# Expert routing moved earlier beside a shared expert, with one multiply moved from VectorE to ScalarE

## The chip, the cores and the metric

One NeuronCore of a Trainium2 chip runs the whole program. The metric is the time of one execution on the device, in microseconds (us); lower is better. A run is the median of several executions.

## What is computed

64 samples of 64 rows and 512 columns (4096 rows, here called tokens, of width 512). First each sample is multiplied by one of 8 matrices and gets a bias; then comes a mixture of experts with a shared expert, and the input is added:

```
h = einsum('bct,bcd->bdt', x, cond_weights[itok]) + fside[itok][:, :, None]   # 64x64 matrices
scores = sigmoid(h @ gate_weight.T)                    # 16 experts
biased = scores + expert_bias
# of 4 groups of 4 experts the 2 with the largest sum of their top two; of those the top 4 experts
w = 2.5 * scores[top4] / sum(scores[top4])
out = x + sum_e w_e * (silu(h @ g_e.T) * (h @ u_e.T)) @ d_e.T     # 4 of 16 experts per token
        + (silu(h @ sg.T) * (h @ su.T)) @ sd.T                    # shared expert, every token
```

The hidden width of each expert is 256. All is float32; a product of the experts is made as three passes over high and low parts.

## The kernel before, in words

A tile is 128 tokens. The program has three stages, and all five engines run written-out instruction lists that meet at semaphores.

**Conditioning stage (some 80 us), loop `for n in range(NT + 2)`, 32 tiles.** GpSimd (POOL) reads two entries of `itok_row` per tile and copies the two 64x64 matrices out of `cond_sb` into `cw_ring` (L526, L534); after tile 4 it makes constants with `late_consts` (L490 and on), among them `token_q`, `lane_q` and `tile_q`. TensorE (PE) multiplies (L755), ScalarE (ACT) adds the bias (L622), SyncE (SP) stores the rows in `h_rows` (L394), PE transposes them (L730), ACT copies the result (L626), PE makes the router's logits (L772). Ahead of it PE runs `WARM_UP` = 8 matmuls on ones (L716). SP issues the first loads in the order `cond_sb`, `itok_row`, others (L375 to L380).

**Shared expert (some 80 to 233 us), steps n = 0 to 31, one tile each.** In step n PE runs `gate_up(n)` (12 matmuls into `psGU`), transposes `hid` of tile n-1 (L730), then whatever the tables of numbers put in this step, then `down(n-2)` (6 matmuls into `psY`). ACT runs `copy_y(n-3)` (L653), `copy_xT(n+1)` (L613), SiLU (L691), `copy_hidT(n-1)` (L644) and, in the steps of `HIGHS`, a high part of a piece of weights (L603). VectorE (DVE) runs `split_x(n+1)` (L1257), then `route_part(n)`, then `mix(n)` (L1280), then `split_hid(n-1)` (L1270).

`route_part` is the routing in 15 numbered parts, one per step, then the reading of two word tables, and then 16 groups of "entries". Each group covers two columns of tokens and takes three VectorE operations on float16: a one-hot of the tile number (`entry`, L1232 by way of L907), a one-hot of the lane (`lane1h`, which lies in `x_ring`, by way of L907), and `entry` times the token number `token_q` (L1235). PE then multiplies `lane1h` by `entry` into the bank `psM` (`fill_slots`, L850), 8 matmuls a group; the sum over all groups is the table of token numbers for each place of each expert tile. `ENTRY_STEPS` says in which step each group is made, 14 to 24, and PE fills it one step later. `fill_idx` (step 25, L1245 and on) turns the table into row indices, `idx_all`. After that POOL gathers rows for the first 14 expert tiles (`gather`, L545), in places that `FIRST_GATHER` = 23 and `GATHERS` set: behind the accumulation of shared tile 23's result into `out` (L558), and so on. Before a gather of tiles 8 and up POOL waits until the shuffle of the tile that used its buffer has landed.

SP has one queue. In it stand the loads of the experts' weights, 1.5 MB each (`load_raw`, L399), whose places `RAW_LOADS` sets and which wait for the low parts (`LOWS`, VectorE, L1240) of the weights that they overwrite; and the shuffles (L415 and L418), which bring gathered rows, two tiles at a time, into the layout that VectorE's transposition `turn_x` (L1264) reads. ACT's queue has the copies of x into `out` (`copy_x`, L597), 1 MB each.

**Routed experts (some 233 to 858 us).** 143 tiles in a loop with the same step, weights of 16 experts one after another; results are scattered with addition (L550).

The word tables (which weights each engine prepares when) are made by PE as sums into `psM` (L784, L801, L802) and read by VectorE (L1176, L1177, L1181). Since they use the bank of the fill, the first fill has to wait until they are read.

## Time and profile before

| what | us |
|---|---|
| median of 3 runs | 878.07 (875.76 to 878.13) |
| the profiled execution's own time | 876.7 |
| its span | 875.0 |
| TensorE busy in the span | 854.5 |
| VectorE, ScalarE, GpSimd busy | 497.5, 401.8, 439.8 |

The profile is of one execution. The span runs from its first to its last instruction; the 1.7 us around it are launch and end. In rows of the page and of the trace "busy" is time inside instructions, overlapping ones counted once; what stands behind an arrow in brackets released the engine after it had been idle. PE's matmuls are pipelined, so that its rows overlap.

### The profile page before, as it was taken

To read this page: it belongs to the slowest core of one execution; us is meant where nothing else is said; L and a number is where in the kernel's file an instruction comes from. 1 tells how busy PE (TensorE), PEld (TensorE's weight loads), DVE (VectorE), ACT (ScalarE), POOL (GpSimd) and SP (SyncE) were. 2 spreads that over 40 slices of the span, in tenths; PEclk is the share of its full clock that TensorE was granted. 3 is DMA by queue.
4 is the path that set the end of the run, shared out by engine and by line. 5 is a ranking of instruction groups with operands and counts; after the bars stand their busy time and mean duration, and the time that the engine had idled before them with its cause. 6 is when DMAs were issued, how large, how long until landed. Compare 5 with 4: busy or idle time off the path is not lost.

```text
span 875.0 us, 19555 instructions
## 1 busy us (share of the span) xinstructions
PE 854.5 (98%) x4136; PEld 693.9 (79%) x4137; DVE 497.5 (57%) x1071; ACT 401.8 (46%) x852; POOL 439.8 (50%) x402
## 2 busy tenths in 40 slices
PE   8999999999899999999999999999999999999994
PEld 6778887888788888888888888888878878887883
DVE  1457677886464454564446644756647456464540
ACT  4675443534443333553445534645545355453331
POOL 4430211115446656656656647656656575765333
PEclk8999999999999999999999999999999999999998
DMA  7983576758999999989999999999898999999644
GB/s 235 345 291 133 134 126 170 173 98 207 262 241 263 218 180 197 183 200 285 226 187 173 204 268 214 184 298 232 197 275 174 280 241 235 240 183 193 119 61 62
DMA packets 147092, 179.06 MB, mean 205 GB/s; under 512 B 30986, under 2 KB 104210, under 8 KB 144658
## 3 DMA queue, kind: packets, MB, share of 16 engines
q0 software_dynamic: 37296, 86.95, 50.3%
q1 hardware_dynamic: 108258, 80.41, 35.7%
q10 hardware_dynamic: 1408, 10.49, 3.5%
q14 instruction: 112, 0.92, 0.4%
q8 instruction: 18, 0.29, 0.1%
HBM read 82.48 MB, written 65.04 MB: 169 GB/s over the span
## 4 chain that ended last, share of the span: by engine, by line
PE 79%; DMA 7%; issue 5%; SPq 3%; POOL 2%; DVE 0%; ACT 0%; POOLq 0%; DVEq 0%; ACTq 0%
PE psGU L824 44%; PE psY L824 22%; PE psY L755 4%; PE psH L730 4%; PE psGU L772 3%; DMA out<-y_ring,idx_all 3%; DMA tok_ring<-h_rows,idx_all 2%; SPq L415 2%; PE psT L730 2%; DMA w_ring<-tok_ring 2%; POOL out L550 1%; POOL out L558 1%; SPq L418 0%; PE psM L850 0%; SPq L436 0%
## 5 line engine op out<-in xcount | busy, mean ns | idle before, releaser
L824 PE MATMUL psGU<-split_w,xT_hi 128*128 (+1 forms) x1400 | 433.2, 391 | 3.3 <-DVE xT_lo L1257 3.3
L550 POOL DMA_INDIRECT out<-y_ring,idx_all x143 | 234.8, 1642 | 207.4 <-SPq L454 190.1
L824 PEld LDWEIGHTS psGU<-split_w,xT_hi 128*128 128x128 f32 x1400 | 263.0, 188 | 61.1 <-issue 5.3
L824 PE MATMUL psGU<-split_w,xT_lo 128*128 (+1 forms) x700 | 274.1, 392 | 0.0
L824 PE MATMUL psY<-split_w,hidT_hi 128*128 (+1 forms) x700 | 233.0, 414 | 0.2 <-issue 0.2
L691 ACT ACTIVATE aT<-psGU 128x256 f32<-128x256 f32 x175 | 67.3, 385 | 264.0 <-PE psGU L824 262.4
L1257 DVE TENSOR_TENSOR xT_lo<-psT,xT_hi 128x512 fp32r<-128x512 f32 x143 | 98.8, 691 | 148.0 <-ACT xT_hi L613 133.7
L545 POOL DMA_INDIRECT tok_ring<-h_rows,idx_all x143 | 147.7, 1033 | 52.9 <-issue 43.2
L653 ACT ACTIVATE y_ring<-psY 128x512 f32<-128x512 f32 x175 | 104.0, 594 | 143.9 <-PE psY L824 127.3
L824 PEld LDWEIGHTS psGU<-split_w,xT_lo 128*128 128x128 f32 x700 | 131.7, 188 | 28.0
L824 PE MATMUL psY<-split_w,hidT_lo 128*128 (+1 forms) x350 | 138.2, 395 | 0.0
L824 PEld LDWEIGHTS psY<-split_w,hidT_hi 128*128 128x128 f32 x700 | 118.5, 189 | 16.2 <-issue 0.7
L1282 DVE SCALAR_TENSOR_TENSOR aT<-aT,w_ring,psGU 128x256 f32<-128x256 f32 x143 | 66.9, 468 | 86.7 <-ACT aT L691 86.7
L1264 DVE STREAM_TRANSPOSE psT<-x_ring 128x512 f32<-128x512 f32 x143 | 102.5, 717 | 6.1 <-DMA w_ring<-tok_ring 6.1
L558 POOL DMA_DIRECT2D out<-y_ring x32 | 28.2, 882 | 131.8 <-ACT y_ring L653 131.7
L613 ACT ACTIVATE xT_hi<-psT 128x512 fp32r<-128x512 f32 x143 | 84.7, 592 | 5.2 <-DVE psT L1264 5.2
L824 PEld LDWEIGHTS psY<-split_w,hidT_lo 128*128 128x128 f32 x350 | 65.8, 188 | 15.0
L1297 DVE TENSOR_TENSOR split_w<-raw_w,split_w x42 | 51.5, 1227 | 41.1 <-ACT split_w L663 38.2
L1270 DVE TENSOR_TENSOR hidT_lo<-psH,hidT_hi 128x256 fp32r<-128x256 f32 x175 | 73.1, 417 | 1.0 <-ACT hidT_hi L644 1.0
L730 PEld LDWEIGHTS psH<-ident,aT 128*128 128x128 f32 x350 | 48.9, 140 | 26.0 <-DVE aT L1280 2.8
L730 PE MATMUL psH<-ident,aT 128*128 128x128 f32 x350 | 66.9, 272 | 2.4 <-DVE hidT_lo L1270 2.4
L644 ACT ACTIVATE hidT_hi<-psH 128x256 fp32r<-128x256 f32 x175 | 66.4, 379 | 1.7 <-PE psH L730 1.7
(177 smaller groups left out, 488.9 us busy)
## 6 DMA issues: line engine op xcount, KB each, us to landing
x_ring<-tok_ring SPq DMA_DIRECT2D x284, 128.0 KB
raw_w<-ffn_w SPq DMA_DIRECT2D x17, 1536.0 KB, 11.7
h_rows<-tok_ring SPq DMA_DIRECT2D x32, 256.0 KB, 3.6
out<-y_ring POOLq DMA_DIRECT2D x32, 256.0 KB
x_ring<-x SPq DMA_DIRECT2D x24, 256.0 KB, 4.6
tok_ring<-h_rows,idx_all POOLq DMA_INDIRECT x143
out<-y_ring,idx_all POOLq DMA_INDIRECT x143
x_ring<-x ACTq DMA_DIRECT2D x8, 256.0 KB, 3.7
```

Source lines behind the costliest of these rows:

```text
L545: pool.indirect_dma_start(tok_ring[:, r % RING, :], None, h_rows[:, :], bass.IndirectOffsetOnAxis(idx_all[:, r:r + 1], 0)).then_inc(gather ...
L550: pool.indirect_dma_start(out[:, :], bass.IndirectOffsetOnAxis(idx_all[:, r:r + 1], 0), y_ring[:, r % YRING, :], None, compute_op=ALU.add) ...
L613: act.activation(xT_hi[:, t.slot % 2, :], xT, ACT.Copy).then_inc(xhi_ready, 1)
L644: act.activation(hidT_hi[:, t.slot % 2, :], psH[:, 0:I], ACT.Copy).then_inc(hidhi_ready, 1)
L653: act.activation(y_ring[:, s, :], psY[t.slot % 2][:], ACT.Copy).then_inc(y_ready, 1)
L691: act.activation(silu[:, t.slot % 2, :], psGU[t.slot % 2][:, 0:I], ACT.Silu).then_inc(silu_ready, 1)
L730: mm = pe.transpose(dst[:, k * P:(k + 1) * P], src[:, k * P:(k + 1) * P], ident[:])
L824: mm = pe.matmul(dst, a[:, slot, c], w(at + col + k * H), start=(k == 0 and a is high and at == 0), stop=(k == parts - 1 and a is low))
L1257: v.tensor_tensor(xT_lo[:, t.slot % 2, :], xT, xT_hi[:, t.slot % 2, :].bitcast(F32), ALU.subtract).then_inc(xT_ready, 1)
L1264: v.transpose(psT[t.slot % 2][:].rearrange("p (k b j) -> p k j b", k=HK, j=QUADS), x_duo[:, t.slot // DUO_TILES, :, t.slot % DUO_TILES, :] ...
L1270: v.tensor_tensor(hidT_lo[:, t.slot % 2, :], psH[:, 0:I], hidT_hi[:, t.slot % 2, :].bitcast(F32), ALU.subtract).then_inc(hidT_ready, 1)
L1282: ins = v.scalar_tensor_tensor(out=hid[:, half, :], in0=gate, scalar=w_ring[:, w_slot, bass.ds(expert, 1)], in1=up, op0=ALU.mult, op1=ALU. ...
```

## The change

`route_part` now takes its work from `ROUTE_STEPS`, by name: the same parts in fewer steps, and the parts that lead to the tokens' places (`slots`, `top_slots`, `places`) come ahead of those that lead to the words. The 16 groups of entries are made in steps 9 to 20. The multiplication by token numbers leaves VectorE: ScalarE scales the lane one-hots, two activations a group (`scale_lanes`), with a column of `token_no` as scale. The word tables use the banks `psT[0]` and `psT[1]`. `fill_idx` is in step 22, the gathers begin behind shared tile 20, low parts and weight loads have other steps, `WARM_UP` is 12, and SP loads `itok_row` ahead of `cond_sb`.

```diff
+ROUTE_STEPS = {0: ("groups",), 1: ("top_experts",), 2: ("ties", "counts"), 3: ("weights",), 4: ("ranks",),
+               5: ("take_turns",), 6: ("starts",), 7: ("slots", "keys"), 8: ("top_slots",), 9: ("places",),
+               10: ("words",), 11: ("columns",), 12: ("tables",), 14: ("read_words",), 15: ("read_sp_words",),
+               22: ("fill_idx",)}
-ENTRY_STEPS = {14: (0,), 15: (1, 2), 16: (3,), 17: (4, 5), 18: (6,), 19: (7, 8), 20: (9,), 21: (10, 11),
-               22: (12,), 23: (13, 14), 24: (15,)}
-FILL_IDX = 25
+ENTRY_STEPS = {9: (0,), 11: (1,), 13: (2, 3), 14: (4,), 15: (5,), 16: (6, 7), 17: (8, 9), 18: (10, 11), 19: (12, 13),
+               20: (14, 15)}
-PE_POS_FFN = {1: 2, 4: 3}
-PE_WORDS, READ_WORDS = 12, 13
-PE_SP_WORDS, READ_SP_WORDS = 13, 14
+PE_POS_FFN = {1: 2, 3: 3}
+PE_WORDS = 13
+PE_SP_WORDS = 14
-LOWS = {25: ((1, 0),), 26: ((1, 1), (1, 2)), 27: ((2, 0),), 29: ((2, 1),), 31: ((2, 2),)}
-RAW_LOADS = {14: 1, 15: 2, 23: 3, 28: 4}
-WARM_UP = 8
+LOWS = {21: ((1, 0),), 23: ((1, 1),), 24: ((1, 2),), 26: ((2, 0),), 29: ((2, 1),), 31: ((2, 2),)}
+RAW_LOADS = {14: 1, 15: 2, 23: 3, 31: 4}
+WARM_UP = 12
-FIRST_GATHER = 23
-GATHERS = {23: (0, 1), 24: (2, 3), 25: (4, 5), 26: (6, 7), 28: (8, 9), 29: (10, 11), 30: (12, 13)}
+FIRST_GATHER = 20
+GATHERS = {20: (0, 1), 21: (2, 3), 22: (4, 5), 23: (6, 7), 25: (8, 9), 26: (10, 11), 27: (12, 13)}
...
-            sp.dma_start(cond_sb[:], cond_w).then_inc(cond_loaded, 16)
             sp.dma_start(itok_row[:], itok.unsqueeze(0)).then_inc(itok_loaded, 16)
+            sp.dma_start(cond_sb[:], cond_w).then_inc(cond_loaded, 16)
...
-                iota(token_q[:, 0:half, :], [[P, half], [0, TOPK]], -N // 2, 1)
-                iota(token_q[:, half:NT, :], [[P, half], [0, TOPK]], 1, 1)
+                iota(token_no[:, 0:half], [[P, half]], -N // 2, 1)
+                iota(token_no[:, half:NT], [[P, half]], 1, 1)
...
-                elif n in (NT - 1, NT):
-                    copy_xT(tile_at(n - (NT - 1)), n - (NT - 1))
+                if n in (NT - 2, NT - 1):
+                    copy_xT(tile_at(n - (NT - 2)), n - (NT - 2))
...
+            def scale_lanes(g):
+
+                act.wait_ge(places_ready, 2 * (g + 1))
+                s = g % ENTRY_RING
+                half = PAIRS // DUO // ENTRIES
+                for k in range(ENTRIES):
+                    lanes = lane1h[:, s, k * half:(k + 1) * half, :, :].rearrange("p d l q -> p (d l q)")
+                    act.activation(lanes, lanes, ACT.Copy, scale=token_no[:, g * ENTRIES + k:g * ENTRIES + k + 1]
+                                   ).then_inc(entry_ready, 1)
...
                     copy_hidT(t + -1, None if n is None else n - 1)
+                for g in ENTRY_STEPS.get(n, ()):
+                    scale_lanes(g)
...
-                pe.wait_ge(words_ready, 1)
-                pe.wait_ge(order_ready, 1)
-                pe.matmul(psM[0:1, 0:NRP], e_cols[:, USED:USED + 1], first[:], start=True, stop=False)
+                pe.matmul(psT[1][0:1, 0:NRP], e_cols[:, USED:USED + 1], first[:], start=True, stop=False)
...
-                pe.wait_ge(entry_ready, g + 1)
+                pe.wait_ge(entry_ready, ENTRIES * (g + 1))
                 if g == 0:
-                    pe.wait_ge(sp_words_ready, 1)
+                    pe.wait_ge(pos_read, NB)
...
-                tokens = token_q[:].rearrange("p c k -> p (c k)")[:, pairs]
-                tt(entry[:, s], every(tile_q[:]), duos(slot_tile[:, pairs], NRP), ALU.is_equal)
-                tt(lane1h[:, s], every(lane_q[:]), duos(slot_lane[:, pairs], P), ALU.is_equal)
-                settle()
-                v.tensor_tensor(entry[:, s], entry[:, s], duos(tokens, NRP), ALU.mult).then_inc(entry_ready, 1)
+                v.tensor_tensor(entry[:, s], every(tile_q[:]), duos(slot_tile[:, pairs], NRP), ALU.is_equal
+                                ).then_inc(places_ready, 1)
+                v.tensor_tensor(lane1h[:, s], every(lane_q[:]), duos(slot_lane[:, pairs], P), ALU.is_equal
+                                ).then_inc(places_ready, 1)
```

On ScalarE, step 17 of the shared expert before (the first row is `copy_y`, `xT_hi` is `copy_xT`, the row with `aT` is SiLU, `split_w` a high part):

```order
L653 ACTIVATE y_ring<-psY 128x512 [waits scattered2,down_done]
L613 ACTIVATE xT_hi<-kept_w 128x512 [waits gu_done]
L691 ACTIVATE aT<-psGU 128x256 [waits hid_ready,gu_done]
L644 ACTIVATE hidT_hi<-psH 128x256 [waits down_done,hid_xposed]
L603 ACTIVATE split_w<-raw_w 128x1024 [waits xT_ready,raw_loaded]
L597 DMA out<-x 16x16384
```

The same step now, number 17, with two groups to scale:

```order
L656 ACTIVATE y_ring<-psY 128x512 [waits scattered2,down_done]
L616 ACTIVATE xT_hi<-kept_w 128x512 [waits gu_done]
L704 ACTIVATE aT<-psGU 128x256 [waits hid_ready,gu_done]
L647 ACTIVATE hidT_hi<-psH 128x256 [waits down_done,hid_xposed]
L689 ACTIVATE x_ring<-x_ring,token_no 128x512 [waits places_ready]
L689 ACTIVATE x_ring<-x_ring,token_no 128x512
L689 ACTIVATE x_ring<-x_ring,token_no 128x512 [waits places_ready]
L689 ACTIVATE x_ring<-x_ring,token_no 128x512
L606 ACTIVATE split_w<-raw_w 128x1024 [waits xT_ready,raw_loaded]
L600 DMA out<-x 16x16384
```

Four activations, the first of each pair behind a wait for VectorE (`places_ready`), now stand between `copy_hidT` and the high part, and so ahead of the next step's `copy_y` and `copy_xT`.

On VectorE, a step with two groups before (`xT_lo` is `split_x`, the row with `aT` is `mix`):

```order
L1257 TENSOR_TENSOR xT_lo<-kept_w,xT_hi 128x512 [waits xhi_ready]
L907 TENSOR_TENSOR entry<-tile_q,slot_tile 128x1152 [waits table_done]
L907 TENSOR_TENSOR x_ring<-lane_q,slot_lane 128x1024
L1235 TENSOR_TENSOR entry<-entry,token_q 128x1152 [waits dve]
L907 TENSOR_TENSOR entry<-tile_q,slot_tile 128x1152 [waits table_done]
L907 TENSOR_TENSOR x_ring<-lane_q,slot_lane 128x1024
L1235 TENSOR_TENSOR entry<-entry,token_q 128x1152 [waits dve]
L1280 TENSOR_TENSOR aT<-aT,psGU 128x256 [waits hid_xposed,silu_ready]
```

And now:

```order
L1269 TENSOR_TENSOR xT_lo<-kept_w,xT_hi 128x512 [waits xhi_ready]
L1244 TENSOR_TENSOR entry<-tile_q,slot_tile 128x1152 [waits table_done]
L1246 TENSOR_TENSOR x_ring<-lane_q,slot_lane 128x1024
L1244 TENSOR_TENSOR entry<-tile_q,slot_tile 128x1152 [waits table_done]
L1246 TENSOR_TENSOR x_ring<-lane_q,slot_lane 128x1024
L1292 TENSOR_TENSOR aT<-aT,psGU 128x256 [waits hid_xposed,silu_ready]
```

The multiplication is gone, and with it the wait for the operation before it. There are six steps of this kind in a table that had five, and five of them, 16 to 20, follow on one another.

## Rows read from the trace of the kernel before

**Rows 1.** Waits, whole span: who waited for whom, total us, times, longest

```profile
DVE psT L1264 <- DMA w_ring<-tok_ring: 6.1, 1, 6.1
```

**Rows 2.** Chain that ended last, 205 to 245 us: start, us, what

```profile
216.35 13.74 DMA w_ring<-tok_ring
...
231.70 0.41 PE psH L730 x2
...
233.97 3.86 PE psGU L824 x12
```

**Rows 3.** Stretches: PE busy (instructions), granted clock, DMA share, GB/s

```profile
222.00:229.00 7.00, 7.00 (x33) 1.00 1.10 256
229.00:232.00 3.00, 0.59 (x5) 1.00 1.23 201
...
233.00:236.00 3.00, 3.00 (x9) 0.50 1.24 222
```

**Rows 4.** Timelines of POOL and SP around the gathers, and issues to landing

```profile
207.19 1.11 POOL L545 DMA_INDIRECT tok_ring<-h_rows,idx_all  x1 [0.54 <-issue]
...
210.37 0.34 SPq L399 DMA_DIRECT2D raw_w<-ffn_w  x1
...
out<-x ACTq DMA_DIRECT2D x1, 5.6
```

**Rows 5.** Groups of ScalarE and VectorE, shared expert: busy, mean ns

```profile
L653 ACT ACTIVATE y_ring<-psY 128x512 f32<-128x512 f32 x28 | 16.8, 600 | 34.5 <-PE psY L824 34.5
L613 ACT ACTIVATE xT_hi<-kept_w 128x512 fp32r<-128x512 f32 x24 | 15.0, 623 | 0.0
...
L603 ACT ACTIVATE split_w<-raw_w 128x1024 fp32r<-128x1024 f32 x5 | 5.3, 1061 | 0.0
...
L1235 DVE TENSOR_TENSOR entry<-entry,token_q 128x1152 f16<-128x1152 f16 x16 | 12.1, 758 | 0.6
```

**Rows 6.** ScalarE's bias activation, whole span: min/median/max ns

```profile
L622 ACT ACTIVATE tok_ring<-psY,bias_tok x32: 678/687/691, 8.7 to 78.1; 128x512 f32<-128x512 f32 x32
```

**Rows 7.** VectorE's timeline in one step with two groups

```profile
159.68 0.69 DVE L1257 TENSOR_TENSOR xT_lo<-kept_w,xT_hi 128x512 fp32r<-128x512 f32 x1 [0.90 <-ACT xT_hi L613]
160.29 0.75 DVE L907 TENSOR_TENSOR entry<-tile_q,slot_tile 128x1152 f16<-128x1152 f16 x1
...
162.36 0.75 DVE L907 TENSOR_TENSOR entry<-tile_q,slot_tile 128x1152 f16<-128x1152 f16 x1
```

**Rows 8.** Tile 17's split on VectorE and its products in the chain; SiLU of tiles 16, 17

```profile
155.37 0.68 DVE L1257 TENSOR_TENSOR xT_lo<-kept_w,xT_hi 128x512 fp32r<-128x512 f32 x1
...
158.50 2.72 PE psGU L824 x12
...
155.73 0.38 ACT L691 ACTIVATE aT<-psGU 128x256 f32<-128x256 f32 x1 [1.61 <-PE psGU L824]
...
161.26 0.39 ACT L691 ACTIVATE aT<-psGU 128x256 f32<-128x256 f32 x1 [1.61 <-PE psGU L824]
```

**Rows 9.** Chain at the start: start, us, what

```profile
1.28 3.13 DMA itok_row<-itok
...
6.29 1.10 PE psY L755 x2
...
10.21 0.85 PE psT L730 x4
...
19.21 0.95 PE psY L755 x2
```

**Rows 10.** Timelines at the start: PE's warm-up, ScalarE, POOL

```profile
1.26 3.40 PE L716 MATMUL psM<-ones 128*128 128x128 f32 x16 [1.26 <-DVE ones L928]
...
8.69 0.69 ACT L622 ACTIVATE tok_ring<-psY,bias_tok 128x512 f32<-128x512 f32 x1
...
17.36 0.52 POOL L534 COPY cw_ring<-cond_sb 64x64 f32 x2 [1.36 <-issue]
```

**Rows 11.** Stretches at the start: PE busy, clock, DMA share, GB/s

```profile
8.00:9.00 1.00, 1.00 (x2) 0.50 0.69 264
```

More of the change, by code:

```diff
@@ L311, in build @@
         sp_words_ready = sem("sp_words_ready")
+        places_ready = sem("places_ready")
         entry_ready = sem("entry_ready")
@@ L373, in _ @@
         def _(sp):
+            sp.dma_start(itok_row[:], itok.unsqueeze(0)).then_inc(itok_loaded, 16)
             sp.dma_start(cond_sb[:], cond_w).then_inc(cond_loaded, 16)
-            sp.dma_start(itok_row[:], itok.unsqueeze(0)).then_inc(itok_loaded, 16)
             sp.dma_start(itok8[:], itok.partition_broadcast(NS)).then_inc(fside_loaded, 16)
@@ L783, in sums @@
                     for k, (column, rows_e) in enumerate(terms):
-                        mm = pe.matmul(psM[0:1, at:at + rows_e.shape[1]], column, rows_e[:, :],
+                        mm = pe.matmul(psT[0][0:1, at:at + rows_e.shape[1]], column, rows_e[:, :],
                                        start=(k == 0), stop=(k == len(terms) - 1))
@@ L1175, in read_words @@
                 v.wait_ge(words_summed, 1)
-                v.tensor_copy(order[:], psM[0:1, 3 * NR:3 * NR + E + SPLITS + 2]).then_inc(order_ready, 1)
-                v.tensor_copy(words[:], psM[0:1, 0:3 * NR]).then_inc(words_ready, 1)
+                v.tensor_copy(order[:], psT[0][0:1, 3 * NR:3 * NR + E + SPLITS + 2]).then_inc(order_ready, 1)
+                v.tensor_copy(words[:], psT[0][0:1, 0:3 * NR]).then_inc(words_ready, 1)
             def read_sp_words():
                 v.wait_ge(sp_words_summed, 1)
-                put(v.tensor_copy(sp_rows[:], psM[0:1, 0:NRP]))
+                put(v.tensor_copy(sp_rows[:], psT[1][0:1, 0:NRP]))
                 settle()
@@ L1193, in token_slots @@
                 in_batches = slot_e[:].rearrange("p (b c e) -> p b c e", c=BC, e=E)
-                ts(start, start, float(P), 1.0, ALU.mult, ALU.add)
+                ts(first_slot[:], start, float(P), 1.0, ALU.mult, ALU.add)
                 settle()
-                tt(per_chunk(slot_e[:], E), per_chunk(pos[:], E), over_chunks(start, NT), ALU.add)
+                tt(per_chunk(slot_e[:], E), per_chunk(pos[:], E), over_chunks(first_slot[:], NT), ALU.add)
                 settle()
@@ new lines, in route_part @@
+                for part in ROUTE_STEPS.get(n, ()):
+                    if part == "groups":
+                        route_groups(NB - 1)
+                    elif part == "top_experts":
+                        top_experts(NB - 1)
+                    elif part == "ties":
+                        chosen_experts(NB - 1)
+                    elif part == "counts":
+                        read_positions(NB - 2)
+                        count_slots(NB - 1)
+                    elif part == "weights":
+                        route_weights(NB - 1)
+                    elif part == "ranks":
+                        expert_ranks()
+                    elif part == "take_turns":
+                        expert_turns()
+                    elif part == "starts":
+                        expert_starts()
+                    elif part == "slots":
+                        token_slots()
+                    elif part == "keys":
+                        expert_keys()
+                    elif part == "top_slots":
+                        top_slots()
+                    elif part == "places":
+                        slot_places()
+                    elif part == "words":
+                        expert_words()
+                    elif part == "columns":
+                        expert_columns()
+                    elif part == "tables":
+                        tile_tables()
+                    elif part == "read_words":
+                        read_words()
+                    elif part == "read_sp_words":
+                        read_sp_words()
+                    elif part == "fill_idx":
+                        fill_idx()
```

44 lines of the change are left out of this document (3 added, 41 removed).

## The prediction

> **What bounds the kernel now.** I read in the order: busy shares, waits, the chain of waits, then timelines of the places that the chain names. TensorE is busy 854.5 of 875.0 us, so only what TensorE itself does, its half-speed time, and the few places where it stands still can change the time. Two of these lie where the change works.
>
> The first is the passage from the shared expert to the routed ones. VectorE waits 6.1 us, once, for the shuffle of the first gathered pair [rows 1]; in the chain that shuffle (its last DMA, `w_ring<-tok_ring`) takes 13.74 us from issue at 216.35 to landing at 230.1, and TensorE starts again at 231.70 [rows 2]. In the stretch 229 to 232 TensorE is busy 0.59 of 3.00 us: it stands 2.4 us. Behind that the granted clock is 0.50 (1.2 GHz) in 233 to 236, and full before [rows 3]; the 12 products at 233.97 take 3.86 us where 2.73 is usual [rows 2]. Against an even step of 4.34 us the SiLUs of tiles 31 and 32 come 2.1 us late each, **4.2 us** in all, of which half is the wait and half the clock.
>
> Why does the shuffle land so late? SP issued a 1.5 MB load of weights at 210.37 [rows 4], and the shuffle stands behind it in SP's queue. From that issue to the landing it is 19.7 us. The first gather was issued at 207.19 [rows 4].
>
> The second place is the start. TensorE's warm-up ends at 4.66 [rows 10], the first product starts at 6.29 [rows 9], and the clock, full until then, is 0.50 in 8 to 9 [rows 11]. Four transposes take 0.85 there [rows 9]; at full clock they take 0.44. The gap of 1.6 us before the first product is what went ahead of the fall.
>
> **The change, part by part.**
>
> *Earlier gathers, loads and shuffles.* The places are ready in `fill_idx` of step 22 instead of 25, and the first gather stands behind shared tile 20 instead of 23: three steps of 4.34 us or a little over, so the gather goes at about 194 to 195. The weight load that goes ahead of the shuffle waits for the last low part of turn 1, now in step 24 instead of 26: some 10 us earlier, near 200. With the same 19.7 us the shuffle lands near 220. It meets more traffic now: the last 1 MB copy of x, which took 5.6 us [rows 4] and was over before the load, now runs beside it. So 220 to 226. VectorE could use it late by 2.4 us less than it did before without TensorE stopping, that is until 227.7, and until 228.8 with the delay found below. The wait goes, and the half clock with it: **-4.2 us**; bounds 0 (lands as late as before) and -4.2. The next thing that could be late is the following pair, needed two steps (8.7 us) later, which lands some 2 us behind the first.
>
> *Multiply from VectorE to ScalarE.* VectorE is spared 16 x 758 ns [rows 5], but it was not the bound: in a two-group step it was about as long as TensorE. ScalarE gets 32 activations of 128x512. Their price is not in the trace. From below: a plain copy from the same memory, 623 ns. From above: an activation that also reads a column of numbers per partition, 687 ns [rows 6], taken without any overlap. Consecutive ones overlap by 0.1 us, so I take 0.59 us each (687 less 0.1), since this one reads such a column too; ends 0.52 and 0.69. The Trainium skill ("ScalarE: Activation LUTs", What ACT_TABLE_LOAD costs) gives 186 ns plus 0.833 ns an element and 93 ns more for each column operand, and an overlap of 93 ns back to back. By that, as an estimate, one would take 0.61 us and the sum would be 0.2 us higher; the plain copy's 623 ns agrees with it (613).
>
> What counts is not the sum but a ring of waits, new in this kernel: `split_x` on VectorE, then the two groups, then ScalarE's scaling of the second group, its high part, `copy_y`, `copy_xT`, and `split_x` again. The split is 0.61 us; a group of three operations took 2.07 [rows 7], without the multiply 1.35, so two are 2.70; two scalings 1.18; the high part 0.95 (1061 ns less the overlap); `copy_y` 0.49 and `copy_xT` 0.53 [rows 5]; semaphores 0.2. That is **6.66 us** with a high part (steps 17, 18, 19) and 5.7 without (steps 16 and 20). TensorE's step with two fills takes 5.5 us (SiLU 155.73 to 161.26 [rows 8]). The ring falls behind by 3 x 1.2 + 2 x 0.2 = 3.9 us. The cover is what a split is ahead of its product: tile 17's ended at 156.0 and its product began at 158.50 [rows 8], 2.5 us, up to 2.8 after steps with fewer groups. So TensorE waits about 1.2 us near step 20: **+1.2 us**. With 0.52 the lag is about 2.6 and nothing is left; with 0.69 it is near 5.8 and 3.4 us are left. These waits are shorter each than the one that went ahead of a fall of the clock.
>
> *Steps merged, tables in other banks.* VectorE's heaviest early steps (`ties` with `counts`, 3.4 us of work; `slots` with `keys`, 2.8) stay inside 4.34 us with the 1.3 us of split, mix and split. TensorE does the same 128 fill matmuls and the same sums; I cost this at nothing. What hides it is VectorE's lead; without that an overlong step would cost its excess, at most 0.4 us. The order of experts is read one step later, so the first weight load is too, some 5 us; it landed 7 us before ScalarE's first use, and 2 to 3 us are left.
>
> *Accumulations behind gathers.* POOL's gathers of tiles 8 to 13 wait for shuffles, and now stand ahead of the accumulations of shared tiles 26, 27 and 28 instead of 29 to 31. Normal if the shuffles land by about 226; costed at nothing (rival D).
>
> *Start.* The DMA of `itok_row` took 3.13 us for 0.2 KB [rows 9]; it stood behind 256 KB in the same queue. First in it, it lands perhaps 0.9 us earlier, and POOL's copies with it. Four more warm-up matmuls take 0.4 us at half clock, 0.2 at full: TensorE is busy until 5.3 to 6.4, about where the first product starts, so the gap that went ahead of the fall closes. If the clock then stays up, the first transposes start not at 10.21 but when ScalarE's first tile is done, at 9.4 (8.69 + 0.69 [rows 10]), and tile 5 could start at 16.4 instead of 19.21 [rows 9]: 2.8 us. But POOL made tile 5's matrices only from 17.36 to 17.88 [rows 10], behind its constants; with 0.9 us from the load and 0.3 from shorter constants that is 16.7, so 2.4 us at most. A new gap opens (TensorE waits for ScalarE's first tile from 8.0 to 9.4), so the clock may fall anyway, later. I take **-1.9 us**, between 0 and -2.8.
>
> Sum: -4.2 + 1.2 - 1.9 = -4.9 us, from 876.7 of the profiled execution to 871.8. That execution is below the median of the runs (878.07); the mean of the four times is 877.2. I move the result by half a microsecond and more to that: **872.4 us**. All cases below are moved by the same 0.6. About 0.3% (2.6 us) is what a measurement of this kernel can tell from no change.
>
> **Rivals.**
>
> A. *The start gives nothing*: the clock falls all the same, or POOL's constants hold tile 5. For it: the new gap before the first transposes. Against: TensorE's clock was full through the warm-up. 876.7 - 4.2 + 1.2 + 0.6 = 874.3. Chance 0.15.
>
> B. *The ring of waits costs its upper end*, 3.4 us: 876.7 - 4.2 + 3.4 - 1.9 + 0.6 = 874.6. The Trainium skill's table (same page, Rules for kernel authors) says to multiply on VectorE and not on ScalarE; the trace has the price of the exchange, one operation of 758 ns for two of some 690. Chance 0.12.
>
> C. *The shuffle is still late*, at 230, because copy, gathers and load share the DMA engines (share already 1.10 in 222 to 229 [rows 3]). One microsecond of wait and the half clock stay, 3.1 of 4.2: 875.5. Chance 0.08.
>
> D. *Slower: POOL's accumulations are held up.* If the shuffle lands at 232 or later, gather 8 holds the accumulation of tile 26; issued 3 us and landed 9 us after the shuffle, at 241, it is late for `copy_y` of tile 30, which needs its buffer near 236.5, and TensorE stands twice, each time with a half clock after it: 3.2 + 2.1, then 2.3 + 2.1, in all 9.7 in place of 4.2. 876.7 + 5.5 + 1.2 - 1.9 + 0.6 = 882.1. It decides from a landing at 232. For it: 8 MB in 30 us. Against: the load starts 10 us earlier. Chance 0.04.
>
> E. *Both small terms at their good ends* (ring 0, start -2.8): 870.3. Chance 0.11.
>
> **How the numbers follow.** The forecast (871 to 874) has 0.5. The range 869.0 to 876.5 takes in A, B, C and E with a microsecond for how runs differ, and leaves out D and a part of the tails. Faster by over 0.3% (under 875.4): all but D, half of C and parts of A and B, 0.84. Within 0.3%: 0.12. Slower: 0.04.
>
> **What would show it.** After the change VectorE's transposition no longer waits for `w_ring<-tok_ring` near 225, and the clock is full from 20 to the last tiles. TensorE stands about 1 us around step 20 (180 to 186), released by VectorE, with `split_x` waiting for ScalarE's `copy_xT`. The first gather is near 193, the shuffle lands before 227. The fifth tile of conditioning starts near 17. Wrong would be: a wait at the passage that stays, waits of ScalarE's `copy_y` for `out` near 236, or TensorE waits in steps 13 to 20 of more than 3 us.

## The result and the profile after

The change made the kernel faster: median **872.52 us** (869.14 to 877.28, 17 runs) against 878.07 us (873.78 to 884.29, 17 runs). The ratio is 0.9939, with a 95% interval of 0.9914 to 0.9963. The profiled execution has an own time of 872.52 us and a span of 870.8 us, 4.2 us below that of before in both.

The head of the page after:

```profile
span 870.8 us, 19587 instructions
...
PE 851.7 (98%) x4144; PEld 691.9 (79%) x4145; DVE 484.6 (56%) x1055; ACT 421.2 (48%) x884; POOL 440.2 (51%) x402
```

TensorE is still the bound. It is busy 2.8 us less than before for nearly the same instructions, so part of the gain is time at the full clock. The rest is time in which it no longer stands.

Stretches of the kernel after (columns: stretch, PE busy, PEld, DVE, ACT, POOL, granted clock, DMA share, GB/s):

```profile
8.00:11.00 3.00, 2.83 (x13) 1.48 (x13) 2.30 (x12) 2.54 (x6) 1.97 (x9) 1.00 1.01 363
...
180.00:190.00 10.00, 9.32 (x54) 7.30 (x53) 8.13 (x17) 6.09 (x13) 2.31 (x3) 1.00 0.62 142
...
229.00:232.00 3.00, 3.00 (x15) 2.47 (x14) 1.60 (x3) 2.45 (x5) 2.40 (x3) 1.00 1.10 294
...
233.00:236.00 3.00, 3.00 (x16) 2.50 (x15) 1.70 (x5) 2.63 (x5) 1.56 (x3) 1.00 1.03 310
```

Against [rows 3]: in 229 to 232 TensorE is now busy all 3.00 us, and the clock is full in 233 to 236. Against [rows 11]: the clock stays full behind 8, though TensorE is idle for 0.2 us of 8 to 11. In 180 to 190 it is idle for 0.7 us, which is the ring of waits, below.

The passage after: VectorE's timeline, then POOL's and SP's.

```profile
222.85 0.69 DVE L1269 TENSOR_TENSOR xT_lo<-kept_w,xT_hi 128x512 fp32r<-128x512 f32 x1 [1.57 <-issue]
223.46 0.72 DVE L1276 STREAM_TRANSPOSE psT<-x_ring 128x512 f32<-128x512 f32 x1
```

```profile
193.61 1.65 POOL L548 DMA_INDIRECT tok_ring<-h_rows,idx_all  x1 [0.53 <-DMA out<-y_ring]
...
221.84 1.06 POOL L548 DMA_INDIRECT tok_ring<-h_rows,idx_all  x1 [7.00 <-DMA w_ring<-tok_ring]
...
224.43 1.01 POOL L561 DMA_DIRECT2D out<-y_ring  x1
```

```profile
199.99 0.35 SPq L402 DMA_DIRECT2D raw_w<-ffn_w  x1
200.55 3.08 SPq L418 DMA_DIRECT2D x_ring<-tok_ring  x4
203.68 3.77 SPq L421 DMA_DIRECT2D w_ring<-tok_ring  x1
```

The 6.1 us of [rows 1] are gone: the transposition follows the split without a wait. The first gather is issued at 193.61, the weight load at 199.99, and gather 8, which waits for the shuffle, goes at 221.84. So the shuffle landed near 221.8, which is 21.8 us after the load's issue (before: 19.7).

The start after, in the chain:

```profile
1.26 5.37 PE psM L731 x24
6.64 0.86 PE psY L770 x2
...
9.28 0.66 PE psT L745 x4
...
16.41 0.72 issue
17.13 1.10 PE psY L770 x2
```

The warm-up ends where the first product starts, and the first transposes start at 9.28 instead of 10.21. Tile 5 starts at 17.13 instead of 19.21 [rows 9], after a stop of 0.7 us.

The ring of waits, first on VectorE, then on ScalarE, then TensorE's waits in 85 to 240 us:

```profile
173.45 0.69 DVE L1269 TENSOR_TENSOR xT_lo<-kept_w,xT_hi 128x512 fp32r<-128x512 f32 x1 [2.69 <-ACT xT_hi L616]
...
180.03 0.69 DVE L1269 TENSOR_TENSOR xT_lo<-kept_w,xT_hi 128x512 fp32r<-128x512 f32 x1 [2.68 <-ACT xT_hi L616]
```

```profile
175.45 2.60 ACT L689 ACTIVATE x_ring<-x_ring,token_no 128x512 f16<-128x512 f16 x4 [1.49 <-DVE x_ring L1246]
177.96 1.04 ACT L606 ACTIVATE split_w<-raw_w 128x1024 fp32r<-128x1024 f32 x1
...
179.38 0.62 ACT L616 ACTIVATE xT_hi<-kept_w 128x512 fp32r<-128x512 f32 x1
```

```profile
PE psH L745 <- DVE hidT_lo L1282: 0.5, 2, 0.3
PE psGU L837 <- DVE xT_lo L1269: 0.4, 1, 0.4
```

From split to split 6.58 us pass in a step with two groups and a high part, each split waiting 2.7 us for `copy_xT` behind ScalarE's scalings. TensorE waits for VectorE three times, at 177.5, 180.8 and 184.1 in steps 20 and 21, 0.9 us in all.

**One ruler for all kernels.** TensorE paces the SiLUs of `gate_up`, so the starts of three of them part the first quarter of the program. The SiLU of shared tile 0 shows the start, that of tile 29 the steps with fills, that of the first routed tile the passage. These are the three rows of the kernel after (ScalarE's timeline):

```profile
82.62 0.38 ACT L704 ACTIVATE aT<-psGU 128x256 f32<-128x256 f32 x1 [1.14 <-PE psGU L837]
...
220.11 0.38 ACT L704 ACTIVATE aT<-psGU 128x256 f32<-128x256 f32 x1 [1.61 <-PE psGU L837]
...
233.08 0.39 ACT L704 ACTIVATE aT<-psGU 128x256 f32<-128x256 f32 x1 [1.64 <-PE psGU L837]
```

The same rows of every profiled execution, in us; the last column is the time from the third row to the end of the span:

| Kernel | SiLU of tile 0 | from there to tile 29 | from there to routed tile 0 | from there to the end |
|---|---|---|---|---|
| before | 84.5 | 136.1 | 17.2 | 637.1 |
| before again (e12) | 88.8 | 136.1 | 15.2 | 639.0 |
| after | 82.6 | 137.5 | 13.0 | 637.7 |
| e1, warm-up 8 | 82.9 | 137.6 | 13.1 | 639.0 |
| e2, matrices loaded first | 83.3 | 137.3 | 13.0 | 636.8 |
| e3, multiply on VectorE | 82.8 | 135.6 | 13.0 | 634.3 |
| e4, high parts moved | 82.9 | 135.8 | 13.0 | 636.5 |
| e5, gathers late | 82.4 | 137.3 | 13.0 | 635.4 |
| e6, before, load later | 88.5 | 136.1 | 13.0 | 642.7 |
| e7, constants later | 81.8 | 137.2 | 13.0 | 635.8 |
| e8 = e4 and e7 | 81.9 | 135.6 | 13.0 | 636.5 |
| e9, before, warm-up 12 | 83.2 | 136.0 | 15.5 | 635.5 |
| e10 = e1 and e2 | 86.0 | 137.3 | 13.0 | 635.8 |
| e11 = e3 and e7 | 81.8 | 135.6 | 13.0 | 638.0 |

Each column moves only with the part of the program that it spans. Between before and after it is -1.9, +1.4 and -4.2 us, together -4.8 at the first routed tile; the routed stage gave back 0.6. That last column varies by up to 4.7 us between kernels whose routed stage is the same, so no part of a result is read from it.

**The clock of the runs.** Each timed run has a span and a mean granted clock too, and (1 - clock) x span is the clock time that it was not granted. Not all of that is a loss. In every profile the clock also falls once TensorE has made its last product (in after the products end at 859.6 and the half clock begins at 863.1), and this end alone is 3.8 us of the figure in after, which is all that its profile has, and 3.2 to 4.9 us in the others. So only differences between kernels say something, and they do not say where in the program the clock fell.

| Kernel | runs | mean clock (lowest to highest) | not granted |
|---|---|---|---|
| before, beside e1 to e11 | 73 | 0.9920 (0.986 to 0.994) | 7.0 us |
| after | 17 | 0.9946 (0.992 to 0.996) | 4.7 us |
| e1 to e5, e7, e8, e11 together | 68 | 0.9946 (0.991 to 0.997) | 4.7 us |
| e6 | 10 | 0.9921 (0.988 to 0.994) | 6.9 us |
| e10 | 12 | 0.9929 (0.992 to 0.994) | 6.2 us |
| e9 | 10 | 0.9900 (0.985 to 0.996) | 8.8 us |

Two more runs of before, over 1.5% above its fastest, are left out. The means of the times differ by 4.3 us (877.0 for the 73 of before, 872.8 for the 17 of after, not all on one chip); 2.4 us of that is clock. Of the 73 runs of before 23 have a clock of 0.991 or less and average 880.4 us, the other 50 average 875.5; none of the 17 runs of after is that low.

### The profile page after: what moved, and what is told of

Same layout as the page of the kernel before. It is cut to its first block, busy times and chain, and to the rows that moved or that the text cites. A ratio compares the mean times of both kernels' runs of the same rounds, so it can differ in the third digit from the quotient of the medians.

```text
span 870.8 us, 19587 instructions
## 1 busy us (share of the span) xinstructions
PE 851.7 (98%) x4144; PEld 691.9 (79%) x4145; DVE 484.6 (56%) x1055; ACT 421.2 (48%) x884; POOL 440.2 (51%) x402
## 4 chain that ended last, share of the span: by engine, by line
PE 85%; issue 4%; DVE 2%; ACT 2%; DMA 2%; SPq 1%; POOL 1%; DVEq 1%; ACTq 0%
PE psGU L837 48%; PE psY L837 24%; PE psH L745 4%; PE psY L770 3%; PE psGU L787 3%; DMA out<-y_ring,idx_all 2%; PE psT L745 2%; POOL out L553 1%; SPq L418 1%; ACT x_ring L689 1%; DVE entry L1244 1%; PE psM L731 1%; DVE x_ring L1246 1%; ACT y_ring L656 0%; ACT xT_hi L616 0%
## 5 line engine op out<-in xcount | busy, mean ns | idle before, releaser
L548 POOL DMA_INDIRECT tok_ring<-h_rows,idx_all x143 | 150.2, 1051 | 57.6 <-issue 42.6
L837 PE MATMUL psY<-split_w,hidT_lo 128*128 (+1 forms) x350 | 137.6, 393 | 0.0
```

Source lines behind the costliest of these rows:

```text
L548: pool.indirect_dma_start(tok_ring[:, r % RING, :], None, h_rows[:, :], bass.IndirectOffsetOnAxis(idx_all[:, r:r + 1], 0)).then_inc(gather ...
L837: mm = pe.matmul(dst, a[:, slot, c], w(at + col + k * H), start=(k == 0 and a is high and at == 0), stop=(k == parts - 1 and a is low))
```

## The experiments

### The start: warm-up and the order of two loads

One reading has to be put right first. The clock's column shows 1.00 from the start of the span, but the trace's first record of the clock comes only at 4.1 us in before, 6.4 in after and 12.8 in e10; what the column shows ahead of it was not measured. Durations were: the warm-up's matmuls in before and in e10 (lowest, median and highest ns):

```profile
L716 PE MATMUL psM<-ones x16: 274/421/579, 1.3 to 4.4; 128*128 128x128 f32 x16
```

```profile
L731 PE MATMUL psM<-ones x16: 421/421/582, 1.3 to 4.6; 128*128 128x128 f32 x16
```

One takes 274 ns at full clock; the median of the warm-up is 421 in every profile. So all these kernels begin at half clock, and it comes up within the first microseconds, in e10 only at 12.8. In before it is up at 4.1 and falls at 7.5, behind the stop of 1.6 us.

The change makes two edits at the start. The first two runs undo one each, in the changed kernel.

```diff
-WARM_UP = 12
+WARM_UP = 8
```

> The changed kernel with 8 warm-up matmuls instead of 12. Theory (the four more matmuls close the gap ahead of the first product, and that keeps the clock up): TensorE idles some 0.5 to 1 us after the warm-up, which is less than before the change (1.6), because itok_row now comes first; if that is still too much, the clock falls to 0.5 within the first 15 us and tile 5 of conditioning starts near 19 instead of 17.1, +1.5 to +2 us on the span's passage to the shared expert. Rival (the earlier matrices did it, not the warm-up): the clock stays full and tile 5 starts at 17.1 as in the changed kernel, no difference.

Measured: 872.01 us (868.89 to 875.62), ratio to before 0.9941 (0.9908 to 0.9974). TensorE's timeline of e1:

```profile
5.38 1.41 PE L770 MATMUL psY<-x_ring,cw_ring 128*128 128x512 f32 x2 [0.34 <-POOL cw_ring L537]
```

The matrices are there at 5.4, so that even the short warm-up leaves a gap of only 0.3 us, and the clock is full from 6.0 us on. Tile 0's SiLU comes 0.2 us later than in the kernel after.

```diff
-sp.dma_start(itok_row[:], itok.unsqueeze(0)).then_inc(itok_loaded, 16)
 sp.dma_start(cond_sb[:], cond_w).then_inc(cond_loaded, 16)
+sp.dma_start(itok_row[:], itok.unsqueeze(0)).then_inc(itok_loaded, 16)
```

> The changed kernel with the load of cond_sb ahead of itok_row again, 12 warm-up matmuls kept. Theory (the warm-up holds the first product back anyway, but POOL's copies set when tile 5 can start): POOL's first copy goes back from 4.45 to 5.6 us, its copy for tile 5 from 16.5 to some 17.2 to 17.6, and tile 5's product from 17.1 to about 18; the clock stays full. +0.7 to +1.1 us. Rival (constants are behind a wait that the swap does not move, or the longer stop at tile 5 lets the clock fall): 0, or +2.5 or more.

Measured: 871.71 us (868.64 to 875.08), ratio 0.9936 (0.9904 to 0.9968). POOL's first copy goes at 5.55 instead of 4.45 and tile 5's matrices come later too: TensorE stops 1.3 us before tile 5 and does it at 17.84. The 12 warm-up matmuls run until the first product starts, and the clock is full from 6.1 us on. Tile 0's SiLU is 0.7 us later.

In these two profiles either edit alone was enough for a full clock. The changed kernel without both is e10:

```diff
-WARM_UP = 12
+WARM_UP = 8
-sp.dma_start(itok_row[:], itok.unsqueeze(0)).then_inc(itok_loaded, 16)
 sp.dma_start(cond_sb[:], cond_w).then_inc(cond_loaded, 16)
+sp.dma_start(itok_row[:], itok.unsqueeze(0)).then_inc(itok_loaded, 16)
```

> The changed kernel with both edits of the start undone: 8 warm-up matmuls and cond_sb loaded first. Theory (either edit alone keeps TensorE's gap ahead of the first product short; with neither the gap of 1.6 us is back): the clock falls to 0.5 somewhere in the first 25 us and the first SiLU of the shared expert comes at 84.5 or later instead of 82.6; passage and ring of waits as in the changed kernel. Median 1.5 to 3 us above the changed kernel. Rival (the fall is chance and has nothing to do with the gap): clock full, first SiLU at 83.3 or less, same time as the changed kernel.

Measured: 875.02 us (871.68 to 877.93), ratio 0.9947 (0.9922 to 0.9973). The chain at its start:

```profile
6.24 2.04 PE psY L770 x2
...
11.28 0.85 PE psT L745 x4
```

After a wait of 1.2 us two products take 2.0 us where 0.95 is usual, and four transposes 0.85 where 0.44 is: half clock until 12.8 us. Against the expectation it did not fall: no warm-up matmul is faster than 421 ns, so it had not come up yet. By the chains this costs 1.7 us up to tile 6 (its products start at 21.20 instead of 19.46). Tile 0's SiLU comes 3.3 us later than in the kernel after, and the other 1.6 us are a second stretch at half clock, from 81.1 to 84.5, with no stop of TensorE ahead of it (stretch, PE busy, granted clock, DMA share, GB/s):

```profile
78.00:81.00 3.00, 2.99 (x29) 1.00 1.11 350
81.00:84.00 3.00, 3.00 (x11) 0.51 0.30 87
```

What brought that one on is open. Without it the SiLU would have come near 84.4, just under the 84.5 that was expected. The 12 timed runs have clocks of 0.992 to 0.994, on average 1.5 us more not granted than the runs of after. They do not show where: in the profiled one the mean clock holds the stretch at 81 and not the start, which lies ahead of the first record. The two ratios, 0.9947 and 0.9939, are too close to be told apart by themselves.

The mirror image is the kernel before with the long warm-up:

```diff
-WARM_UP = 8
+WARM_UP = 12
```

> The kernel before with 12 warm-up matmuls instead of 8, nothing else. Theory (the gap of 1.6 us between warm-up and first product went ahead of the fall of the clock; filling it is enough): the clock stays full in the first 20 us, tile 5 of conditioning starts near 18 (held by POOL) instead of 19.2, -1.2 us. Rival (it took the earlier itok_row): the clock falls as before and tile 5 starts at 19.2 or later.

Measured: 879.05 us (871.81 to 884.63), ratio 1.0027 (0.9992 to 1.0062). In the profile it did what was expected: tile 0's SiLU at 83.2, full clock at the start. But that execution (871.81 us, clock 0.996) was the fastest of ten, and the other nine have clocks of 0.985 to 0.993. The expectation holds for the start of one execution and fails for the time. No run shows where the nine lost theirs.

The kernel before, unchanged, was looked at once more:

> The kernel before, unchanged, for a second profile of its start and of its passage. Theory: the clock falls to 0.5 somewhere in the first 25 us, first SiLU at 84 to 89; VectorE waits 4 us or more for the first shuffle, which lands near 230 behind a weight load of 210, and TensorE stands 2 us or more. Rival (the first profile was a chance): clock full and first SiLU at 83.3 or less; or no stop at the passage.

Measured: 880.85 us. Stretches and chain of e12 at the start:

```profile
14.00:18.00 4.00, 2.46 (x17) 1.83 (x16) 0.00 (x0) 1.78 (x5) 2.31 (x3) 1.00 0.87 267
18.00:20.00 2.00, 1.62 (x6) 1.12 (x7) 0.00 (x0) 0.44 (x1) 0.91 (x4) 0.82 0.22 80
20.00:24.00 4.00, 4.00 (x14) 2.86 (x13) 0.00 (x0) 1.20 (x4) 1.76 (x9) 0.50 0.37 131
...
28.00:32.00 4.00, 4.00 (x27) 3.48 (x25) 0.00 (x0) 2.41 (x5) 0.93 (x4) 0.81 1.01 347
```

```profile
16.45 1.92 issue
```

Here the clock did not fall at the front. It fell after the stop of 1.9 us at tile 5, where POOL's matrices come late, and stayed down until 29.5 (0.81 in 28 to 32). So before has two places at its start at which the clock can go, and in this execution the second cost more (SiLU at 88.8) than the first did in the other (84.5). e6, another kernel with before's start, shows the same fall after 2.0 us. At the front the clock stayed full in both, behind stops of 1.4 us (e12) and 0.8 us (e6), though the program up to there is before's. So the same start goes differently from one execution to the next, and one profile each of e1, e2, e9 and e10 fits the account of the gap but does not prove it.

### POOL's constants

If the stop at tile 5 is POOL's constants, starting them three tiles later must close it.

```diff
-PAIR_TABLES = 4
+PAIR_TABLES = 7
```

> The changed kernel with POOL's constants made after tile 7's matrices instead of after tile 4's. Theory (POOL's 7 us of constants hold tile 5 by 0.7 us): POOL has tiles 5 to 7 ready by 12.5, tile 5 starts at 16.4 instead of 17.1, tile 8 waits only for its buffer, and the first SiLU of the shared expert comes 0.7 us earlier. Rival (tile 8 is now held by the same 7 us): TensorE waits at tile 8, and nothing is won.

Measured: 870.94 us (867.53 to 873.71), ratio 0.9947 (0.9921 to 0.9972). Chain of e7:

```profile
16.50 0.95 PE psY L770 x2
```

Tile 5 follows the tile before it without a stop, and tile 0's SiLU is 0.8 us earlier, as expected. The last two of these constants are the dear ones: in e8's POOL timeline `lane_q` takes 1.53 us and `tile_q` 1.68.

### The ring of waits

Two ways out of it: give VectorE its multiply back, or take two high parts out of the steps with two groups.

```diff
-v.tensor_tensor(lane1h[:, s], every(lane_q[:]), ..., ALU.is_equal).then_inc(places_ready, 1)
+tt(lane1h[:, s], every(lane_q[:]), ..., ALU.is_equal)
+settle()
+v.tensor_tensor(entry[:, s], entry[:, s], duos(tokens, NRP), ALU.mult).then_inc(entry_ready, 1)
...
-                for g in ENTRY_STEPS.get(n, ()):
-                    scale_lanes(g)
```

> The changed kernel with the multiplication by token numbers back on VectorE (three operations a group there, none on ScalarE), all places of the steps kept. Theory (the ring of split, groups, scaling, high part, copy_y, copy_xT sets 6.6 us a step in steps 17 to 19): without scaling the ring is 0.61 + 4.15 + mix and split 0.67 = 5.4 us on VectorE, under TensorE's 5.45, so the 1.3 us of TensorE's waits near step 20 go; the span is 1.3 us shorter. Rival (VectorE is now the bound, five two-group steps in a row have no light step between them): TensorE waits for VectorE in steps 17 to 20 and the span is the same or up to 1.5 us longer.

Measured: 869.93 us (867.02 to 876.78), ratio 0.9927 (0.9888 to 0.9966). In e3 TensorE has no wait in 85 to 240 us, and from tile 0 to tile 29 it takes 135.6 us instead of 137.5. The split after a step with two groups does not wait for ScalarE:

```profile
176.05 0.68 DVE L1258 TENSOR_TENSOR xT_lo<-kept_w,xT_hi 128x512 fp32r<-128x512 f32 x1
```

```diff
-HIGHS = {17: (1, 0), 18: (1, 1), 19: (1, 2), 24: (2, 0), 28: (2, 1), 31: (2, 2)}
+HIGHS = {17: (1, 0), 21: (1, 1), 22: (1, 2), 24: (2, 0), 28: (2, 1), 31: (2, 2)}
```

> The changed kernel with two of ScalarE's high parts moved from steps 18 and 19 to 21 and 22, out of the steps with two groups. Theory (the ring of waits): the ring is 6.6 us only in step 17, 5.6 in the others, so it falls behind by 1.1 + 4 x 0.15 = 1.7 us, which the cover of 2.5 us takes; TensorE's 1.3 us of waits go. Rival (the waits come from VectorE's or ScalarE's load and not from their order): TensorE still waits about 1 us between steps 18 and 22.

Measured: 869.28 us (866.75 to 869.95, 4 runs), ratio 0.9882 (0.9828 to 0.9937). VectorE's splits in e4:

```profile
172.77 0.69 DVE L1269 TENSOR_TENSOR xT_lo<-kept_w,xT_hi 128x512 fp32r<-128x512 f32 x1 [1.74 <-ACT xT_hi L616]
...
178.41 0.69 DVE L1269 TENSOR_TENSOR xT_lo<-kept_w,xT_hi 128x512 fp32r<-128x512 f32 x1 [1.74 <-ACT xT_hi L616]
```

The ring is 5.64 us, 0.94 shorter, which is one high part. TensorE has no wait in 85 to 240 us here either. Both ways give back 1.7 to 1.9 us between tiles 0 and 29. So the moved multiply alone did no harm: with the high parts elsewhere it is as quick as on VectorE (135.8 and 135.6).

### The passage: gathers or the weight load

The change moves both forward. e5 puts only the gathers back; the weight load stays early.

```diff
-FIRST_GATHER = 20
-GATHERS = {20: (0, 1), 21: (2, 3), 22: (4, 5), 23: (6, 7), 25: (8, 9), 26: (10, 11), 27: (12, 13)}
+FIRST_GATHER = 23
+GATHERS = {23: (0, 1), 24: (2, 3), 25: (4, 5), 26: (6, 7), 28: (8, 9), 29: (10, 11), 30: (12, 13)}
```

> The changed kernel with the gathers in their old places (first one behind shared tile 23, the next ones as before), low parts and weight loads as changed. Theory (the shuffle was late because the 1.5 MB weight load stood ahead of it in SP's queue; the load goes at 200 now): first gather near 206, shuffle issued near 212 when the load has landed (11 to 12 us after 200), so it lands within 3 to 6 us, by 218, and TensorE does not stop at the passage; same time as the changed kernel. Rival (it was the gathers that were late): the shuffle lands at 226 or later and TensorE stands 1 us or more near 229, with a half clock after it, +3 to +4 us.

Measured: 870.01 us (867.73 to 873.18), ratio 0.9931 (0.9899 to 0.9963). SP's timeline, then VectorE's:

```profile
199.16 0.34 SPq L402 DMA_DIRECT2D raw_w<-ffn_w  x1
213.63 3.46 SPq L418 DMA_DIRECT2D x_ring<-tok_ring  x4
217.13 0.66 SPq L421 DMA_DIRECT2D w_ring<-tok_ring  x1
```

```profile
223.07 0.72 DVE L1276 STREAM_TRANSPOSE psT<-x_ring 128x512 f32<-128x512 f32 x1
```

The first gather goes at 206.26, as late as in the kernel before [rows 4], and the passage is still closed. The shuffle's last part, issued at 217.13, is used without a wait at 223.07: 5.9 us at most, where it took 13.74 before [rows 2]. For the passage the earlier gathers were not needed.

e6 is the converse, on the kernel before: gathers as they were, two loads put later, the first of them behind the first shuffles.

```diff
-RAW_LOADS = {14: 1, 15: 2, 23: 3, 28: 4}
+RAW_LOADS = {14: 1, 15: 2, 26: 3, 31: 4}
```

> The kernel before with one thing changed: SP issues the loads of the third and fourth turn's weights in steps 26 and 31 instead of 23 and 28, so that the third stands behind the first two shuffles instead of ahead of them. Theory (the load ahead in the queue delays the shuffle): the first shuffle is issued near 213 as before, lands by 220 instead of 230, and TensorE's stop at 229 to 231.5 and the half clock at 233 to 236 go: 4.2 us less than the kernel before at the passage. Rival (all DMA queues together are the bound, share 1.1): the shuffle lands at 226 or later and less than 2 us are won.

Measured: 874.36 us (869.95 to 882.02), ratio 0.9978 (0.9946 to 1.0009). SP's timeline, VectorE's, and TensorE's waits in 240 to 300 us:

```profile
219.87 0.66 SPq L418 DMA_DIRECT2D w_ring<-tok_ring  x1
...
227.90 0.35 SPq L399 DMA_DIRECT2D raw_w<-ffn_w  x1
```

```profile
227.96 0.72 DVE L1264 STREAM_TRANSPOSE psT<-x_ring 128x512 f32<-128x512 f32 x1
```

```profile
PE psGU L824 <- issue: 6.4, 2, 3.7
```

The passage is closed here too (13.0 in the table), by moving nothing but loads, though the shuffle was issued 3.5 us later than before (219.87 for 216.35). The gain is lost later: TensorE stands 2.7 us until 272.4 and 3.7 us until 280.7, and after the second stop its clock falls. Both stops are ScalarE's, whose `copy_y` waits for a scatter of results, with `copy_xT` behind it:

```profile
270.36 0.60 ACT L653 ACTIVATE y_ring<-psY 128x512 f32<-128x512 f32 x1 [5.90 <-DMA out<-y_ring,idx_all]
...
278.67 0.60 ACT L653 ACTIVATE y_ring<-psY 128x512 f32<-128x512 f32 x1 [6.67 <-DMA out<-y_ring,idx_all]
```

The first scatter was issued at 264.01 (250.09 in the kernel after), behind gathers that had waited 7.2 us for a shuffle and 9.5 us for an accumulation. That the two loads, 17.5 and 10 us later than before (210.37 and 235.50), are what held these transfers is likely but not shown.

The two runs settle which transfer it is: the 1.5 MB load. The last part of the shuffle takes 13.7 us (before) and 18.1 us (after, 203.68 to 221.8) with the load just ahead, at most 5.9 (e5) and 8.1 us (e6, 219.87 to 227.96) without. How the load delays it is shown in part. The Trainium skill ("DMA: Bandwidth & Descriptors", Queues, rings and completion order) says that each DMA engine takes a queue's descriptors in their order. The trace of before agrees. The queues' traffic in 213 to 217, then in 217 to 230 (packets, MB, share of the 16 engines; q1 is SP's queue, q0 POOL's):

```profile
q1 hardware_dynamic: 107, 1.29, 86.2%
q0 software_dynamic: 40, 0.08, 13.0%
```

```profile
q0 software_dynamic: 1016, 2.59, 82.1%
q1 hardware_dynamic: 1903, 0.81, 26.9%
```

Four parts of the shuffle are issued from 213.37 on, but up to 217 SP's queue moves packets of 12 KB, which are the load's; the shuffle's small ones follow when those are done, at 217.4. Waiting its turn is the smaller piece, though. The shuffle's first packet comes 4.1 us (before) and 5.8 us (after) behind its first issue, against 2.0 in e5 and e6. From its first packet to its last it then takes 12 and 14 us, against 6 and 8, with the load gone from the engines. In before POOL's queue has 82% of them meanwhile (73% in 219 to 227 of e6). Whether transfers that the load had held up come due together there, no run tells apart.

### Versions that are ahead of both at the first routed tile

e8 joins e4's and e7's edits:

```diff
-PAIR_TABLES = 4
+PAIR_TABLES = 7
-HIGHS = {17: (1, 0), 18: (1, 1), 19: (1, 2), 24: (2, 0), 28: (2, 1), 31: (2, 2)}
+HIGHS = {17: (1, 0), 21: (1, 1), 22: (1, 2), 24: (2, 0), 28: (2, 1), 31: (2, 2)}
```

> The changed kernel with both improvements that paid in a profile: two high parts moved to steps 21 and 22, and POOL's constants after tile 7. Theory (the ring of waits and the stop at tile 5 are separate): first SiLU of the shared expert at 81.8 as with the constants alone, lag gone by step 22, so the routed tiles begin 2.1 us earlier than in the changed kernel; 0.9915 to 0.993 of the kernel before. Rival (what is won ahead is lost to the transfers behind): the passage gets a wait again, no better than the changed kernel's 0.994.

Measured: **869.14 us** (866.74 to 874.25) against 879.21 on the same chip, ratio 0.9894 (0.9851 to 0.9936). Tile 0's SiLU at 81.9, tile 29's 135.6 later: routed tile 0 is 2.6 us earlier than in the kernel after, at 230.47.

e11 joins e3's diff (the multiply on VectorE) and e7's:

```diff
-PAIR_TABLES = 4
+PAIR_TABLES = 7
```

> The changed kernel with the multiplication on VectorE and POOL's constants after tile 7. Theory: as the run with both improvements, since either way of breaking the ring takes the same 1.4 to 1.7 us; routed tiles begin 2.1 us or a little more earlier than in the changed kernel; 0.990 to 0.993 of the kernel before. Rival (VectorE at 5.4 of 5.45 us a step has no room left and loses it again): a wait of TensorE for VectorE of 1 us or more in steps 16 to 21.

Measured: 872.03 us (868.07 to 873.35), ratio 0.9903 (0.9866 to 0.9940). Up to routed tile 0 it agrees with e8 within 0.1 us (81.8, 135.6, 13.0). e8 has the lowest ratio but for e4, whose interval holds it. None of these intervals is clear of that of after (0.9914 to 0.9963), so in the whole time no version is shown to be faster than the change.

## Why the prediction was right, point by point

**The sum.** Predicted -4.9 us in the profiled execution; measured -4.8 at the first routed tile, -4.2 at the end. The terms, read in the table's columns: passage -4.2 predicted and -4.2 measured; ring +1.2 and +1.4; start -1.9 and -1.9. The median came out at 872.52 for 872.4; that near is luck, since runs of one kernel differ by 8 us and the terms of before differ between its executions, as below.

**Passage.** Load near 200, first gather at 194 to 195, landing in 220 to 226: measured 199.99, 193.61, 221.8. The x copy that was to slow things did: 5.6 us became 9.1. That the load ahead of the shuffle is the cause is shown by e5 and e6; that standing in its queue is the way is true of a part of the delay. The prediction carried the old 19.7 us over as a whole (21.8 measured) and did not see that they held 12 us in which the load was done. Nor did it separate that the load's place is all that the passage needed: moving the gathers, a large part of the diff, was worth nothing there.

**The size of the passage.** Of the 4.2 us the clock is 1.7 (half clock from 232.8 to 236.2) and the wait the rest. The wait is there in all three profiles with before's passage (e9 stops 2.2 us, e12 2.0), but in those two the clock did not fall behind it, and the passage cost 2.5 and 2.2 us instead of 4.2. So -4.2 is this pair of executions' number, and it came out because the prediction and the table use the same execution of before. Over all runs 2.4 of the 4.3 us are clock, wherever it fell, and 1.9 are left for the stops that are gone, less the ring's.

**Ring.** Predicted 6.66 us, measured 6.58, and it reads off term by term: split 0.61, two groups 2.54, then until the high part 1.36 (predicted 1.18 and 0.2), high part 0.95, `copy_y` 0.47, `copy_xT` 0.65. TensorE's waits, 0.9 us in three pieces, lie in steps 20 and 21, released by VectorE as foreseen; counted by the starts of its products, whose rows overlap, they cost 1.4 us. The scaling was taken at 0.59 each; the four of 175.45 take 2.60 together, 0.65 each, nearer to the upper end. Alone one takes 717 ns (median), above the 687 taken as a bound from above, so that bound was none. An estimate from the figures of the Trainium skill ("ScalarE: Activation LUTs", What ACT_TABLE_LOAD costs) is 706 ns for it; the trace agrees within 11 ns. The ring's sum survived because the two groups took 2.54 us where 2.70 was put down. The term of the forecast, +1.2, is met by +1.4 partly by luck: against the same kernel without the ring (e3) the cost is 1.9 us, and 0.5 of it is made up by what the rest of the change saves in these steps (135.6 in e3, 136.1 in before).

**Merged steps, accumulations.** Costed at nothing. They gave those 0.5 us, for which no run here looked for a cause. POOL's gather 8 waited 7.0 us for the shuffle and the accumulation of tile 26 went at 224.43, without a wait of `copy_y` on TensorE's path.

**Start.** The number was right, the reasons only half. The prediction read the clock as full through the warm-up; its matmuls take 421 ns, so it was at half until 4.1. The gap did close and the clock was full behind it, but in e1 and e2 either edit alone was enough, and in e12 and e6 before's own start kept it too. The fear that the wait of 8.0 to 9.4 would bring the clock down again did not come true. And the stop at tile 5, which the prediction took for a mere delay by POOL's constants, can take the clock with it in the kernel before: after 1.9 us in e12 and 2.0 in e6. The prediction did not see this second fall. Beside e12 the same change would have won 6.2 us at the start instead of 1.9.

**Rivals.** A (start gives nothing) is excluded by the start's columns. B (ring 3.4 us) is too dear by 2. C (shuffle at 230) and D (landing at 232 or later) are excluded by 221.84. E (both small terms good) did not come true in the change; e8 is near it, by its own places of high parts and constants.

**Open.** Why the timed runs of e9 are at a lower clock than before's, while its profiled one is at 0.996, was not found. Nor is it known in which share of before's executions each of its falls occurs, what brought the clock down in e10 at 81 us, and why the shuffle takes twice as long once the load ahead of it is done.

## What to carry to other kernels

When a small transfer lands late, look first at what its own queue carries ahead of it: with the large load out of the way the passage closed, and moving fourteen gathers and their whole preparation added nothing there. Then look at what the moved load meets in its new place (e6). When work goes to another engine, write out the ring of in-order waits through both engines, with every operation that stands in it; here the cure was to move a neighbour (the high part) out of the heavy steps, not to move the multiply back. And read the mean clock of every run, not only the profiled one, less what the idle end of the program puts into it: a stop of 2 us costs its length always and a half-clock stretch sometimes.

## What was not expected of the hardware

- The same stop does not always cost the same. The clock fell after stops of TensorE of 1.6 and 2.4 us (before), 1.9 (e12), 2.0 and 3.7 (e6) and 2.1 (e4, at 655 us); it stayed full after 1.3 (e2), 1.4 (e9), 1.9 (e11, at 646 us), 2.0 (e12's passage), 2.2 (e9's passage) and 2.7 us (e6, at 272). In e10 it fell once with no stop ahead of it.
- The half-clock stretches are not equally long: the one at before's passage cost 1.7 us, while e12's lasted from 19.3 to 29.5.
- The clock's column is no measurement ahead of the trace's first record of the clock: in e10 it reads 1.00 at the start while products take 2.04 us instead of 0.95. Durations of known operations are the safer reading.
- The 73 runs of the unchanged kernel, on three chips, reach from 871.5 to 885.0 us. A third of them have the lowest clocks, and those average 4.9 us more than the rest.
